# A gated-expert block with a LoRA feed-forward: one scale per expert for the gated rows, and another order of the first six items

## The chip, the cores and the metric

One core of a Trainium2 chip. The metric is the device time of one execution, in microseconds (us).

## What is computed

2048 rows x of 512 floats. Each row's token id picks one of four experts; every expert is a 512x512 matrix, used three times (as gate, as up and as down weight):

```python
n = layernorm(x)
z = n @ ct[e].T                        # gate and up weights are the same matrix
y = (silu(z) * z) @ ct[e]
x = x + tanh(g_xattn) * y              # "the gated rows" are silu(z) * z
n2 = layernorm(x)
x = x + tanh(g_ffn) * (n2 @ W_base + b_base + (n2 @ A_s) @ B_s
                       + sum over the top 2 of 6 routed experts of gate * ((n2 @ A_r) @ B_r))
```

The four expert matrices ("ct" in the kernel) come as 4 MB of floats, the feed-forward weights as 1.26 MB ("w") and 0.23 MB ("up").

## The kernel before

Five engines run lists of instructions written out by hand; semaphores tie them together. Each engine issues strictly in the order of its list.

The rows are sorted by expert, in three steps. VectorE counts and ranks the ids, GpSimd and VectorE build one-hot tiles (L1004, L410), and TensorE multiplies them into a table of row numbers (L684, copied at L1007). 16 tiles of 128 rows, and three extra items for experts that begin inside a tile, give 19 items. Item q is gathered by an indirect DMA that GpSimd issues (L404) into its 512 columns of `xg`.

Every float operand is split into a high and a low f16 part, and a product is three passes: hi x hi and hi x lo (L745, 8 matmuls) and lo x hi (L750, 4 matmuls), each 128x512. For this the operands are scaled by powers of two.

An item goes through: statistics on VectorE (`first_rows`: L1032, L1036); `item_root` on GpSimd (L373, L376, L383), which gives 1/sqrt(var) and the centre; `norm` on ScalarE (L538) into h; for items 0 to 5 `transpose_h` on TensorE (L736) with `hT_hi` on ScalarE (L511) and `hT_lo` on VectorE (L1049), from item 6 (`DMA_FROM`) on `h_hi` (L545), `h_lo` (L1054) and a DMA transpose issued by SyncE (L302); `product_z`; `silu_of` on ScalarE (L522); `activate` on VectorE (L1060), which multiplies silu(z), z and a scale and also sums each row; `scale_rows` (L1066 to L1070), which turns the row's sum into one scale per row (and `y_scale`, which takes it out again); `act_hi` on ScalarE (L529) and `act_lo` on VectorE (L1075), which write the split gated rows; a DMA transpose (L306); `product_y`; and `add_product` on VectorE (L1085, L1087), which adds y times `y_scale` to xg. z alternates between two PSUM banks, y between two others; h, silu and act are single buffers. act_split has two, hT and actT three.

Expert matrices: each arrives in `ct_stage` (1 MB, SyncE, L297; the fourth is issued only after the second gather). Its power of two comes from a sum of squares: for expert 0 from ScalarE (L497), for the others from `gram` on TensorE and `trace` on VectorE (L702, L942); `total` (L709) sums over partitions and `ct_scales` (L949 to L955) makes the scale and `z_scale`. Then `ct_hi` (ScalarE, L503) and `ct_lo` (VectorE, L935) write the two f16 halves of each half matrix. `z_scales` (GpSimd, L391 to L398) spreads `z_scale` over items 4 to 18.

The order around the change: GpSimd issues three gathers, then after `item_root(n)` one gather for n = 0, 1, 2 and two for each n from 3 on. From item 6 on TensorE alternates `product_z(q)` and `product_y(q - 2)` in a loop; ScalarE, VectorE and SyncE have loops that match. The feed-forward weights are loaded from ScalarE's queue (L548), into the space of `ct_stage` that the experts have left, at items 3 to 7. In the loop they are squared, scaled and split. After item 18 comes the feed-forward stage, 16 tiles: TensorE runs 24 matmuls (L727, L731) and the small low-rank ones for each.

`keep_warm` (L691) issues matmuls whose result nobody reads. `act_table` loads (L491, L646) switch ScalarE's function table; the last one stands between `silu_of(18)` and `act_hi(18)`.

## Time and profile before

| | |
|---|---|
| times of three runs | 215.31, 216.76, 218.06 us, median 216.76 |
| the profiled execution | 217.67 us, of which the span of instructions is 215.8 us |
| mean granted TensorE clock | 0.97 of full |
| busy in the span | TensorE 187.3 us (87%), VectorE 158.0 (73%), GpSimd 115.8 (54%), ScalarE 113.8 (53%) |

The profiled execution is one of its own, 0.91 us above the median; the span is its part between the first and the last instruction, and 1.87 us lie around it. A timeline row gives start, duration, engine, line and operation; in brackets stands how long the engine was idle before it, and what released it. "PE" is TensorE, "DVE" VectorE, "ACT" ScalarE, "POOL" GpSimd, "SP" SyncE.

### The profile page before, as it was taken

What the parts mean: (1) busy time and instruction counts of PE and PEld (TensorE: products, weight loads), DVE (VectorE), ACT (ScalarE), POOL (GpSimd) and SP (SyncE); (2) the same over time, 40 slices, a digit from 0 to 9 for tenths busy, and PEclk for the clock granted to TensorE, in tenths of its full rate; (3) what the DMA queues carried; (4) which work ended last, traced back from release to release, by engine and by line L of the source; (5) the groups of instructions that cost most, each with busy time, mean ns of one, the idle gap of its engine ahead of it and who ended that gap; (6) DMA issues with size and microseconds to landing.
All of it is one profiled execution on the core that took longest, in us unless ns stands there. A gap on an engine that the chain in (4) does not pass through costs nothing.

```text
span 215.8 us, 3806 instructions
## 1 busy us (share of the span) xinstructions
PE 187.3 (87%) x1076; PEld 109.2 (51%) x1076; DVE 158.0 (73%) x500; ACT 113.8 (53%) x208; POOL 115.8 (54%) x187
## 2 busy tenths in 40 slices
PE   0499686849994999999999999979999999999870
PEld 0374242314442444544444444637787787787650
DVE  4878496494696669999987994749878878876360
ACT  4445535634464567556665752636657757757210
POOL 4666552688768111116787533142677667776421
PEclk9999887879999999999999999999999999999997
DMA  3986103426999994449979976243389788889942
GB/s 104 380 258 234 49 3 97 111 81 110 189 228 285 251 155 97 97 97 164 256 206 231 149 189 172 53 121 75 61 136 149 104 137 130 122 121 142 121 63 86
DMA packets 58771, 31.37 MB, mean 145 GB/s; under 512 B 52049, under 2 KB 52049, under 8 KB 58754
## 3 DMA queue, kind: packets, MB, share of 16 engines
q1 hardware_dynamic: 53232, 16.80, 39.0%
q0 software_dynamic: 4816, 12.85, 27.9%
q10 hardware_dynamic: 706, 1.52, 2.1%
q8 instruction: 8, 0.13, 0.3%
q14 instruction: 9, 0.07, 0.1%
HBM read 10.71 MB, written 7.86 MB: 86 GB/s over the span
## 4 chain that ended last, share of the span: by engine, by line
PE 67%; DVE 10%; POOL 7%; DMA 4%; issue 4%; ACT 3%; POOLq 1%; SPq 1%; DVEq 0%
PE y_ps L745 6%; PE ffn_b L745 6%; PE z_ps L745 6%; PE actT_ps L745 6%; PE ffn_b L727 5%; PE ffn_a L727 5%; PE z_ps L750 3%; PE actT_ps L750 3%; PE y_ps L750 3%; PE ffn_b L750 3%; PE z_ps L727 3%; PE y_ps L727 2%; PE ffn_b L731 2%; PE ffn_a L731 2%; DMA hT<-h_split 2%
## 5 line engine op out<-in xcount | busy, mean ns | idle before, releaser
L461 POOL DMA_INDIRECT out<-scaled,row_index x14 | 22.4, 1597 | 9.1 <-POOL centre L450 4.6
L373 POOL TENSOR_SCALAR var_eps<-item_stats_t 128x1 f32<-128x1 f32 x19 | 6.4, 337 | 38.4 <-DVE item_stats_t L1036 37.8
L529 ACT ACTIVATE act_split<-act,row_scale 128x512 f16<-128x512 f32 x19 | 13.7, 721 | 21.0 <-DVE row_scale L1069 21.0
L745 PE MATMUL z_ps<-ct_split,hT 128*128 (+1 forms) x80 | 20.3, 400 | 4.2 <-DMA hT<-h_split 3.4
L423 POOL DMA_INDIRECT out<-xg,row_index x14 | 15.5, 1110 | 15.7 <-DVE xg L1087 13.1
L404 POOL DMA_INDIRECT xg<-x_rows,row_index x19 | 20.7, 1091 | 4.9 <-issue 3.8
L745 PE MATMUL ffn_b<-ct_split,hT 128*128 (+1 forms) x72 | 19.8, 425 | 3.4 <-DVE ct_split L935 3.4
L538 ACT ACTIVATE h<-xg,item_centre,item_rstd 128x512 f32<-128x512 f32 x18 | 14.5, 805 | 10.8 <-POOL item_centre L383 10.5
L745 PE MATMUL y_ps<-ct_split,actT 128*128 (+1 forms) x80 | 18.9, 379 | 1.1 <-DMA actT<-act_split 1.1
L727 PE MATMUL ffn_b<-w_split,hT 128*128 128x314 f16 x88 | 18.4, 295 | 0.9 <-ACT scaled L578 0.9
L727 PE MATMUL ffn_a<-w_split,hT 128*128 128x316 f16 x88 | 18.8, 298 | 0.0
L745 PE MATMUL actT_ps<-ct_split,actT 128*128 (+1 forms) x72 | 17.0, 379 | 0.0
L554 ACT ACTIVATE h<-xg,centre,rstd 128x512 f32<-128x512 f32 x16 | 12.8, 802 | 7.8 <-POOL centre L450 7.8
L1203 DVE TENSOR_TENSOR h_split<-h,h_split 128x512 f16<-128x512 f32 x16 | 10.7, 667 | 7.1 <-ACT h_split L559 7.1
L745 PEld LDWEIGHTS z_ps<-ct_split,hT 128*128 128x128 f16 x80 | 7.9, 102 | 14.7 <-issue 6.7
L563 ACT ACTIVATE expd<-logits,neg_max 128x6 f32<-128x6 f32 x16 | 4.8, 299 | 19.4 <-DVE neg_max L1221 19.4
L745 PEld LDWEIGHTS ffn_b<-ct_split,hT 128*128 128x128 f16 x72 | 7.6, 107 | 14.5 <-issue 4.3
L443 POOL TENSOR_SCALAR var_eps<-stats 128x1 f32<-128x1 f32 x16 | 7.3, 454 | 13.2 <-DVE stats L1039 13.1
L1075 DVE SCALAR_TENSOR_TENSOR act_split<-act,row_scale,act_split 128x512 f16<-128x512 f32 x19 | 14.1, 744 | 0.0
L745 PEld LDWEIGHTS y_ps<-ct_split,actT 128*128 128x128 f16 x80 | 7.8, 98 | 10.7 <-issue 1.6
L1032 DVE BATCH_NORM_STATS2 bn<-xg 128x6 f32<-128x512 f32 x19 | 13.0, 687 | 0.0
L935 DVE SCALAR_TENSOR_TENSOR ct_split<-ct_stage,ct_scale,ct_split 128x1024 f16<-128x1024 f32 x8 | 10.1, 1273 | 3.0 <-ACT ct_split L503 3.0
(203 smaller groups left out, 480.7 us busy)
## 6 DMA issues: line engine op xcount, KB each, us to landing
ct_stage<-ct SPq DMA_DIRECT2D x4, 1024.0 KB, 7.3
ct_stage<-w_ffn ACTq DMA_DIRECT2D x4, 315.0 KB, 3.7
hT<-h_split SPq DMA_TRANSPOSE x29, 3.4
xg<-x_rows,row_index POOLq DMA_INDIRECT x19, 4.3
actT<-act_split SPq DMA_TRANSPOSE x19, 3.4
out<-xg,row_index POOLq DMA_INDIRECT x16, 3.8
ct_stage<-w_up ACTq DMA_DIRECT2D x1, 224.0 KB
out<-scaled,row_index POOLq DMA_INDIRECT x14
```

Source lines behind the costliest of these rows:

```text
L404: nc.gpsimd.indirect_dma_start(cols(xg, q), None, x, bass.IndirectOffsetOnAxis(row_index[:, q:q + 1], 0)).then_inc(x_landed[q], 16)
L423: nc.gpsimd.indirect_dma_start(out, bass.IndirectOffsetOnAxis(row_index[:, q:q + 1], 0), cols(xg, q), None).then_inc(x2_stored, 16)
L461: nc.gpsimd.indirect_dma_start(out, bass.IndirectOffsetOnAxis(row_index[:, q:q + 1], 0), scaled[t % 3][:], None, compute_op=ALU.add).then_ ...
L529: nc.scalar.activation(act_split[q % 2][:, 0:D], act[:], ACT.Copy, scale=column(row_scale, q)).then_inc(act_hi_ready, 1)
L538: nc.scalar.activation(h[:], cols(xg, q), ACT.Identity, bias=column(item_centre, q), scale=column(item_rstd, q)).then_inc(h_ready, 1)
L554: nc.scalar.activation(h2[:], cols(xg, tile_position(l)), ACT.Identity, bias=centre[:], scale=rstd[:]).then_inc(h2_ready, 1)
L727: nc.tensor.matmul(ps, h2T[turn][:, k], rhs(part), start=(k == 0 and part == 0), stop=False)
L745: nc.tensor.matmul(ps[:], lhs[:, k], expert_weights(key, k, part), start=(k == 0 and part == 0), stop=False)
L750: last = nc.tensor.matmul(ps[:], lhs[:, KC + k], expert_weights(key, k, 0), start=False, stop=(k == KC - 1))
L1032: nc.vector.bn_stats(bn[:], cols(xg, q)).then_inc(bn_ready, 1)
L1075: nc.vector.scalar_tensor_tensor(act_split[q % 2][:, D:], act[:], column(row_scale, q), act_split[q % 2][:, 0:D], ALU.mult, ALU.subtract). ...
L1203: tt(h2_split[l % 3][:, D:], h2[:], h2_split[l % 3][:, 0:D], ALU.subtract).then_inc(h2_lo_ready, 1)
```

## The change

One scale per expert for the gated rows. `activate` multiplies by `act_scale`, a power of two made from the expert's own, and has no row sum; `scale_rows` is gone; `act_hi` and `act_lo` need no scale; `y_scale` comes once, for all items, from four more instructions on GpSimd in `scale_tables` (before: `z_scales`), which now runs after root 4 in place of root 5. `ct_scales` has two instructions in place of five, and `product_scales` makes the two product scales apart from it. `act_scale` of items 4 to 18 comes in one VectorE instruction, `late_act_scales`.

A new order, on all engines, of what comes before the loop. Four gathers are issued before root 0; after the roots 0 to 5 come 0, 1, 3, 3, 0 and 1 gathers, after the later ones two. VectorE builds 12 of the 16 one-hot tiles in place of 11. The first `total` goes to another bank (`hT_ps`) and does not wait for the row table. `transpose_act(q)` from q = 3 on waits until `product_y(q - 3)` is done.

The feed-forward weights get buffers of their own, and SyncE loads them between its transposes. The feed-forward stage and the loop from item 6 are otherwise as before. The diff, cut:

```diff
-w_stage = ct_stage[:, 0:2].rearrange("p s k n -> p (s k n)")[:, 0:KC * WN]
-up_stage = ct_stage[0:LORA + 1, 2, 0, :]
+w_stage = sb("w_stage", [P, KC * WN])
+up_stage = sb("up_stage", [LORA + 1, D])
...
-DVE_ONEHOTS = TPP - 5
+DVE_ONEHOTS = TPP - 4
...
     def transpose_act(q):
         sp.wait_ge(act_lo_ready, q + 1)
+        if q >= 3:
+            sp.wait_ge(y_done, q - 2)
         sp.dma_start_transpose(actT[q % 3][:], act_split[q % 2][:]).then_inc(actT_landed[q % 3], 16)
...
-    for q in range(1, ITEMS + 1):
+    def load_w(k):
+        sp.dma_start(cols(w_stage, k, WN), w_ffn[k * P:(k + 1) * P, :]).then_inc(w_loaded[k], 16)
+    transpose_act(0)
+    load_w(0)
+    transpose_act(1)
+    load_w(1)
+    transpose_act(2)
+    load_w(2)
+    transpose_act(3)
+    transpose_h(DMA_FROM)
+    load_w(3)
+    transpose_act(4)
+    transpose_h(DMA_FROM + 1)
+    sp.dma_start(up_stage[0:LORA], w_up[0:LORA]).then_inc(up_loaded, 16)
+    sp.dma_start(up_stage[LORA:], w_up[LORA:]).then_inc(up_loaded, 16)
+    for q in range(DMA_FROM, ITEMS):
         transpose_act(q - 1)
-        if q == DMA_FROM - 1:
-            transpose_h(DMA_FROM)
-            transpose_h(DMA_FROM + 1)
-        if DMA_FROM <= q < ITEMS - 2:
+        if q + 2 < ITEMS:
             transpose_h(q + 2)
-        if q >= ITEMS - 2:
+        else:
             transpose_h2(q + 2 - ITEMS)
+    transpose_act(ITEMS - 1)
+    transpose_h2(2)
...
+        pool.wait_ge(z_table_ready, 1)
+        nc.gpsimd.tensor_scalar(z_power[:], z_scale[:], 2.0 ** Z_TOP, None, ALU.mult).then_inc(z_table_step, 1)
+        pool.wait_ge(z_table_step, S + 3)
+        nc.gpsimd.tensor_tensor(z_square[:], z_power[:], z_power[:], ALU.mult).then_inc(z_table_step, 1)
+        pool.wait_ge(gate_mask_ready, 1)
+        nc.gpsimd.tensor_tensor(gated_power[:], z_power[:], gate_mask[:], ALU.mult).then_inc(z_table_step, 1)
+        pool.wait_ge(z_table_step, S + 5)
+        nc.gpsimd.tensor_tensor(y_scale[:], z_square[:], gated_power[:], ALU.mult).then_inc(y_scale_ready, 1)
...
     gather(2)
+    gather(3)
...
-        if n == 5:
-            z_scales()
-        for q in range(next_gather, min(ITEMS, next_gather + (2 if n >= 3 else 1))):
+        if n == 4:
+            scale_tables()
+        for q in range(next_gather, min(ITEMS, next_gather + (0, 1, 3, 3, 0, 1)[min(n, 5)] + (n > 5))):
             gather(q)
...
     def act_hi(q):
-        act_e.wait_ge(row_scale_ready, q + 1)
+        act_e.wait_ge(act_ready, q + 1)
         if q >= 2:
             act_e.wait_ge(actT_landed[(q - 2) % 3], landings(0, q - 2))
-        nc.scalar.activation(act_split[q % 2][:, 0:D], act[:], ACT.Copy, scale=column(row_scale, q)
-                             ).then_inc(act_hi_ready, 1)
+        nc.scalar.activation(act_split[q % 2][:, 0:D], act[:], ACT.Copy).then_inc(act_hi_ready, 1)
...
     ct_hi(0, 0)
     ct_hi(0, 1)
     ct_hi(1, 0)
+    ct_hi(1, 1)
     hT_hi(0)
-    ct_hi(1, 1)
+    ct_hi(2, 0)
     norm(1)
-    ct_hi(2, 0)
     hT_hi(1)
+    norm(2)
     silu_of(0)
     ct_hi(2, 1)
     act_hi(0)
-    norm(2)
-    silu_of(1)
     hT_hi(2)
-    act_hi(1)
     norm(3)
     ct_hi(3, 0)
     ct_hi(3, 1)
+    silu_of(1)
+    hT_hi(3)
+    norm(4)
+    act_hi(1)
     silu_of(2)
-    hT_hi(3)
+    hT_hi(4)
     act_hi(2)
-    norm(4)
     silu_of(3)
-    hT_hi(4)
+    norm(5)
     act_hi(3)
-    act_e.wait_ge(ct_lo_ready, 3)
-    load_w(0)
-    norm(5)
     silu_of(4)
     hT_hi(5)
+    norm(6)
     act_hi(4)
-    load_w(1)
-    norm(6)
     h_hi(6)
     silu_of(5)
     norm(7)
+    h_hi(7)
     act_hi(5)
-    h_hi(7)
-    load_w(2)
...
-    pe.wait_ge(rows_ready, 1)
+    def total_of(first, count):
+        return squares_ps[:, TOTALS_AT + first:TOTALS_AT + first + count]
     pe.wait_ge(ct_squared, 2)
-    total(0, 1, ct_squares[:, 0:1], ct_squares[:, S:S + 1])
+    total(first_total_ps[:, 0:1], ct_squares[:, 0:1], ct_squares[:, S:S + 1])
...
     product_z(0, 0, between=lambda: transpose_h(1))
+    gram(3)
     pe.wait_ge(ct_lo_ready, 2)
     product_z(1, 1)
-    gram(3)
+    transpose_h(2)
     pe.wait_ge(traced, 3)
-    total(3, 1, ct_squares[:, 3:4])
-    transpose_h(2)
+    total(total_of(3, 1), ct_squares[:, 3:4])
     pe.wait_ge(ct_lo_ready, 3)
     product_z(2, 2)
-    product_y(0, 0, between=lambda: transpose_h(3))
+    transpose_h(3)
+    product_y(0, 0)
     pe.wait_ge(ct_lo_ready, S)
-    product_z(3, 3)
-    product_y(1, 1, between=lambda: transpose_h(4))
+    product_z(3, 3, between=lambda: transpose_h(4))
     pe.wait_ge(tables_ready, 1)
     keys = {0: 0, 1: 1, 2: 2, 3: 3, 4: key_of(4), 5: key_of(5)}
     product_z(4, keys[4])
-    product_y(2, 2, between=lambda: transpose_h(5))
+    transpose_h(5)
+    product_y(1, 1)
     product_z(5, keys[5])
+    product_y(2, 2)
     product_y(3, 3)
...
-        after(ts(ct_exponent[:, at], squares_ps[:, TOTALS_AT + first:TOTALS_AT + first + count].bitcast(I32),
-                 23, None, ALU.logical_shift_right))
-        after(ts(ct_power[:, at], ct_exponent[:, at], -0.5, S_FIELD, ALU.mult, ALU.add))
-        ts(ct_scale[:, at], ct_power[:, at], 23, None, ALU.logical_shift_left).then_inc(ct_scale_ready, count)
-        dve.wait_ge(ct_scale_ready, first + count)
-        after(ts(ct_inverse[:, at], ct_scale[:, at], -1.0, BITS_OF_ONE_TWICE, ALU.mult, ALU.add))
-        ts(z_scale[:, at], ct_inverse[:, at].bitcast(F32), 2.0 ** -H_POWER, None, ALU.mult
+        after(ts(ct_root[:, at], total.bitcast(I32), 24, 23, ALU.logical_shift_right, ALU.logical_shift_left))
+        ts(ct_scale[:, at], ct_root[:, at], -1.0, float(S_FIELD << 23), ALU.mult, ALU.add
+           ).then_inc(ct_scale_ready, count)
+    def product_scales(first, count):
+        at = slice(first, first + count)
+        ts(z_scale[:, at].bitcast(I32), ct_root[:, at], 1.0, float(Z_FIELD << 23), ALU.mult, ALU.add
            ).then_inc(z_scale_ready, count)
+        ts(act_scale[:, at].bitcast(I32), ct_root[:, at], -1.0, float(ACT_FIELD << 23), ALU.mult, ALU.add
+           ).then_inc(act_scale_ready, count)
+    def late_act_scales():
+        dve.wait_ge(z_table_ready, 1)
+        ts(act_scale[:, S:].bitcast(I32), z_scale[:, S:].bitcast(I32), -1.0,
+           float((ACT_FIELD + Z_FIELD) << 23), ALU.mult, ALU.add).then_inc(act_scale_ready, 1)
...
     def activate(q):
         dve.wait_ge(silu_ready, q + 1)
+        dve.wait_ge(act_scale_ready, min(q, S) + 1)
         if q:
             dve.wait_ge(act_lo_ready, q)
-        nc.vector.scalar_tensor_tensor(act[:], z_banks[q % 2][:], column(z_scale, q), silu[:], ALU.mult,
-                                       ALU.mult, accum_out=column(row_sum, q)).then_inc(act_ready, 1)
-    def scale_rows(q):
-        dve.wait_ge(act_ready, q + 1)
-        ts(column(row_mean, q), column(row_sum, q), 2.0 ** -ROW_POWER, 2.0 ** -100, ALU.mult, ALU.max
-           ).then_inc(row_mean_ready, 1)
-        dve.wait_ge(row_mean_ready, q + 1)
-        nc.vector.reciprocal(column(row_scale, q), column(row_mean, q)).then_inc(row_scale_ready, 1)
-        ts(column(y_scale, q), column(row_mean, q), column(gate_mask, q), column(z_scale, q), ALU.mult, ALU.mult
-           ).then_inc(y_scale_ready, 1)
+        nc.vector.scalar_tensor_tensor(act[:], z_banks[q % 2][:], column(act_scale, q), silu[:], ALU.mult,
+                                       ALU.mult).then_inc(act_ready, 1)
     def act_lo(q):
         dve.wait_ge(act_hi_ready, q + 1)
-        nc.vector.scalar_tensor_tensor(act_split[q % 2][:, D:], act[:], column(row_scale, q),
-                                       act_split[q % 2][:, 0:D], ALU.mult, ALU.subtract
-                                       ).then_inc(act_lo_ready, 1)
+        tt(act_split[q % 2][:, D:], act[:], act_split[q % 2][:, 0:D], ALU.subtract).then_inc(act_lo_ready, 1)
...
     def add_product(q):
         dve.wait_ge(y_done, q + 1)
-        dve.wait_ge(y_scale_ready, q + 1)
+        dve.wait_ge(y_scale_ready, 1)
...
     gates_of_rows()
+    product_scales(0, 1)
     ct_lo(0, 0)
-    first_rows(0)
+    ct_lo(0, 1)
     trace(1)
     trace(2)
-    ct_scales(1, 2, 2)
+    first_rows(0)
+    ct_scales(squares_ps[:, TOTALS_AT + 1:TOTALS_AT + 3], 1, 2, 2)
     first_norm()
     first_rows(1)
-    ct_lo(0, 1)
+    first_rows(2)
+    ct_lo(1, 0)
     hT_lo(0)
-    ct_lo(1, 0)
     ct_lo(1, 1)
+    ct_lo(2, 0)
+    first_rows(3)
+    activate(0)
     hT_lo(1)
-    activate(0)
-    scale_rows(0)
-    first_rows(2)
-    ct_lo(2, 0)
+    trace(3)
     act_lo(0)
-    trace(3)
     ct_lo(2, 1)
-    ct_scales(3, 1, 3)
+    ct_scales(squares_ps[:, TOTALS_AT + 3:TOTALS_AT + 4], 3, 1, 3)
     hT_lo(2)
+    product_scales(1, 3)
+    first_rows(4)
+    ct_lo(3, 0)
     activate(1)
-    scale_rows(1)
-    first_rows(3)
-    act_lo(1)
-    ct_lo(3, 0)
-    first_rows(4)
-    activate(2)
-    scale_rows(2)
     ct_lo(3, 1)
     hT_lo(3)
+    first_rows(5)
+    act_lo(1)
+    activate(2)
+    act_lo(2)
+    hT_lo(4)
+    activate(3)
+    first_rows(6)
+    act_lo(3)
+    late_act_scales()
+    activate(4)
+    hT_lo(5)
     add_product(0)
-    act_lo(2)
-    first_rows(5)
-    activate(3)
-    scale_rows(3)
-    hT_lo(4)
-    first_rows(6)
+    h_lo(6)
     add_product(1)
-    act_lo(3)
-    activate(4)
-    scale_rows(4)
-    hT_lo(5)
     first_rows(7)
+    act_lo(4)
     add_product(2)
-    act_lo(4)
-    h_lo(6)
+    activate(5)
+    h_lo(7)
     first_rows(8)
-    activate(5)
-    scale_rows(5)
-    h_lo(7)
```

## Rows read from the trace of the kernel before

**Rows 1.** Windows by stage: busy us of each engine, clock, DMA share, GB/s
```profile
20.52:67.89 47.37, 35.60 (x159) 16.22 (x159) 32.98 (x76) 23.56 (x33) 29.99 (x44) 0.89 0.51 116
67.89:145.30 77.41, 76.32 (x365) 35.78 (x366) 60.07 (x160) 43.08 (x64) 32.97 (x58) 1.00 0.75 164
145.30:204.00 58.70, 57.81 (x438) 45.31 (x437) 46.39 (x181) 37.09 (x96) 37.05 (x51) 1.00 0.79 118
```

**Rows 2.** Waits of TensorE, 68 us to the end: us in total, times, longest
```profile
PE z_ps L745 <- DMA hT<-h_split: 3.4, 1, 3.4
PE y_ps L745 <- DMA actT<-act_split: 1.1, 1, 1.1
```

**Rows 3.** Timeline of TensorE: start us, us, line, operation, count, idle before it
```profile
35.12 3.26 PE L745 MATMUL z_ps<-ct_split,hT 128*128 128x512 f16 x8 [0.78 <-ACT hT L511]
...
45.94 3.46 PE L745 MATMUL ffn_b<-ct_split,hT 128*128 128x512 f16 x8 [3.36 <-DVE ct_split L935]
...
67.89 1.90 PE L745 MATMUL z_ps<-ct_split,hT 128*128 x8 [3.39 <-DMA hT<-h_split]
...
73.08 1.89 PE L745 MATMUL ffn_b<-ct_split,hT 128*128 x8
...
75.67 1.89 PE L745 MATMUL actT_ps<-ct_split,actT 128*128 x8
```

**Rows 4.** Timeline of VectorE in the start-up, same columns
```profile
19.21 1.25 DVE L935 SCALAR_TENSOR_TENSOR ct_split<-ct_stage,ct_scale,ct_split 128x1024 f16<-128x1024 f32 x1
20.38 0.69 DVE L1049 TENSOR_TENSOR hT<-hT_ps,hT 128x512 f16<-128x512 f32 x1
20.98 2.47 DVE L935 SCALAR_TENSOR_TENSOR ct_split<-ct_stage,ct_scale,ct_split 128x1024 f16<-128x1024 f32 x2
...
27.23 0.75 DVE L1060 SCALAR_TENSOR_TENSOR act<-z_ps,z_scale,silu 128x512 f32<-128x512 f32 x1 [0.63 <-ACT silu L522]
...
28.21 0.16 DVE L1069 RECIPROCAL row_scale<-row_mean 128x1 f32<-128x1 f32 x1
...
28.46 0.68 DVE L1032 BATCH_NORM_STATS2 bn<-xg 128x6 f32<-128x512 f32 x1
```

**Rows 5.** Timeline of GpSimd in the start-up
```profile
21.27 2.23 POOL L383 TENSOR_SCALAR item_centre<-item_stats_t,item_rstd 128x1 f32<-128x1 f32 x1
...
32.95 1.03 POOL L404 DMA_INDIRECT xg<-x_rows,row_index  x1 [0.17 <-issue]
...
39.19 0.26 POOL L383 TENSOR_SCALAR item_centre<-item_stats_t,item_rstd 128x1 f32<-128x1 f32 x1
...
49.89 1.43 POOL L391 TENSOR_SCALAR z_scale_of<-item_key,z_scale 128x15 f32<-128x15 f32 x4
```

**Rows 6.** Timeline of ScalarE in the start-up
```profile
26.51 0.69 ACT L522 ACTIVATE silu<-z_ps,z_scale 128x512 f32<-128x512 f32 x1 [0.64 <-PE z_ps L750]
...
39.48 0.81 ACT L538 ACTIVATE h<-xg,item_centre,item_rstd 128x512 f32<-128x512 f32 x1 [1.98 <-POOL item_centre L383]
40.20 2.17 ACT L503 ACTIVATE ct_split<-ct_stage,ct_scale 128x1024 f16<-128x1024 f32 x2
```

**Rows 7.** The page, section 6: DMA issues, median us to landing
```profile
xg<-x_rows,row_index POOLq DMA_INDIRECT x19, 4.3
actT<-act_split SPq DMA_TRANSPOSE x19, 3.4
```

**Rows 8.** Line L404, 13.3 to 14 us: the gather of item 2
```profile
L404 POOL DMA_INDIRECT xg<-x_rows,row_index x1: 946/946/946, 13.4 to 13.4; - x1
...
DMA to landing us min/median/max: 6.6/6.6/6.6
```

**Rows 9.** Line L306, all transposes of the gated rows: landing
```profile
DMA to landing us min/median/max: 2.7/3.4/6.2
```

**Rows 10.** Timeline of ScalarE at the last expert item
```profile
136.51 1.28 ACT L646 ACT_TABLE_LOAD   x1
137.80 0.72 ACT L529 ACTIVATE act_split<-act,row_scale 128x512 f16<-128x512 f32 x1
```

More of the change, by code:

```diff
@@ L191, in build_block @@
         squares_ps = ffn_a[1]
+        first_total_ps = hT_ps
         TOTALS_AT = 0
@@ L384, in item_root, with scale_tables @@
                                             column(item_rstd, n), ALU.mult, ALU.mult).then_inc(rstd_ready, 1)
-            def z_scales():
+            def scale_tables():
                 pool.wait_ge(z_scale_ready, S)
@@ L425, in store_x2 @@
                 ).then_inc(x2_stored, 16)
[L427 removed]
+            next_gather, next_store = 4, 0
             for n in range(ITEMS):
@@ L704, in gram, with total @@
                 last.then_inc(gram_done, 1)
-            def total(first, count, *parts):
+            def total(to, *parts):
                 for n, part in enumerate(parts):
-                    last = nc.tensor.matmul(squares_ps[:, TOTALS_AT + first:TOTALS_AT + first + count], ones_f32[:],
-                                            part, start=(n == 0), stop=(n == len(parts) - 1))
+                    last = nc.tensor.matmul(to, ones_f32[:], part, start=(n == 0), stop=(n == len(parts) - 1))
                 last.then_inc(ct_totalled, 1)
-            pe.wait_ge(rows_ready, 1)
+            def total_of(first, count):
+                return squares_ps[:, TOTALS_AT + first:TOTALS_AT + first + count]
             pe.wait_ge(ct_squared, 2)
-            total(0, 1, ct_squares[:, 0:1], ct_squares[:, S:S + 1])
+            total(first_total_ps[:, 0:1], ct_squares[:, 0:1], ct_squares[:, S:S + 1])
             gram(1)
@@ L719, in _ @@
             keep_warm(WARM_UP[1])
+            pe.wait_ge(rows_ready, 1)
             pe.wait_ge(traced, 2)
-            total(1, 2, ct_squares[:, 1:3])
+            total(total_of(1, 2), ct_squares[:, 1:3])
             keep_warm(WARM_UP[2])
@@ L943, in trace, with ct_scales @@
                                                ALU.mult, accum_out=column(ct_squares, e)).then_inc(traced, 1)
[L945 removed]
+            def ct_scales(total, first, count, turn):
                 at = slice(first, first + count)
                 dve.wait_ge(ct_totalled, turn)
[L949 to L956 removed]
+                after(ts(ct_root[:, at], total.bitcast(I32), 24, 23, ALU.logical_shift_right, ALU.logical_shift_left))
[4 more added lines that the diff above has]
+                ts(z_scale[:, at].bitcast(I32), ct_root[:, at], 1.0, float(Z_FIELD << 23), ALU.mult, ALU.add
+                   ).then_inc(z_scale_ready, count)
+                ts(act_scale[:, at].bitcast(I32), ct_root[:, at], -1.0, float(ACT_FIELD << 23), ALU.mult, ALU.add
[4 more added lines that the diff above has]
+                   float((ACT_FIELD + Z_FIELD) << 23), ALU.mult, ALU.add).then_inc(act_scale_ready, 1)
             def reach(slots):
@@ L1014, in _ @@
             cp(key_table[:], item_key[:]).then_inc(tables_ready, 1)
-            ct_scales(0, 1, 1)
+            ct_scales(first_total_ps[:, 0:1], 0, 1, 1)
             def gates_of_rows():
@@ L1023, in gates_of_rows @@
                 dve.wait_ge(gates_ready, 1)
-                after(ts(gate_mask[:], gate_mask[:], gates_t[:, 0:1], 2.0 ** H_POWER, ALU.mult, ALU.mult))
+                ts(gate_mask[:], gate_mask[:], gates_t[:, 0:1], 0.5, ALU.mult, ALU.mult).then_inc(gate_mask_ready, 1)
             def item_stats(q):
```

38 lines of the change are left out of this document (12 added, 26 removed).

## The prediction

> **What bounds the kernel now.** First I read busy time by stage. From 67.89 us on TensorE is busy for 76.3 of 77.4 us and then for 57.8 of 58.7 us; between 20.52 and 67.89 us it is busy for only 35.6 of 47.4 us, at a mean clock of 0.89 [rows 1]. The waits of TensorE behind 68 us are 3.4 us once, which ends at 67.89, and 1.1 us near 142 us [rows 2]. So from z6 (the first product of the loop, at 67.89) to the end the kernel is a row of matmuls, and a gain must come from the time at which z6 starts. In the loop a product takes 75.67 - 73.08 = 2.59 us [rows 3]. By 67.89 ten have run (z0 to z5, y0 to y3), 26 us of work.
>
> Then the timelines of the start-up, to see what TensorE waits for. z2 starts at 35.12 behind item 2's transposes, z3 at 45.94 behind the low half of expert 3, both at half clock: 3.26 and 3.46 us for eight matmuls that take 1.89 at full clock [rows 3]. Behind both lies item_root: the gather of item 3 is issued only at 32.95 [rows 5], so its statistics come late and `norm(3)` starts at 39.48; `ct_hi(3)` stands behind it on ScalarE and starts at 40.20 [rows 6]. The start-up is a ring of gather, statistics, root, norm with one gather in each turn.
>
> GpSimd is slow inside that ring. `item_centre` takes 0.26 us when nothing is in its way, and 2.23 us at 21.27, where it ends with the two `ct_lo` that VectorE runs from 20.98 for 2.47 us [rows 4, 5]. The Trainium skill (GPSIMD Engine Reference, "Key points") says that GpSimd shares its SBUF interfaces with VectorE and is in contention with VectorE instructions that have two SBUF inputs; `ct_lo` is one, and the trace agrees. By that page alone GpSimd would run clear of `activate`, which reads a PSUM bank; I can do without it, since the sum below only lets a GpSimd instruction that begins within a `ct_lo` or `act_lo` wait for its end, as in the rows.
>
> **The parts with small effect.** The row table: GpSimd makes four one-hots in place of five, the table is ready some 0.3 us earlier. The first `total` no longer waits for it; with three instructions fewer in `ct_scales`, expert 0's scale is ready about 0.8 us earlier. In the steady loop, VectorE loses the row sum and three short instructions for each item, about 0.5 us of its 5.2, and `act_hi` can start about 0.4 us sooner after `activate` (27.23 + 0.75 to 28.4, past the reciprocal at 28.21 [rows 4]). TensorE bounds that stretch [rows 1], so that is worth nothing there. At item 18, where TensorE does wait for the gated rows (1.1 us [rows 2]), `act_hi` starts at 137.80 because the table load of 1.28 us ends then [rows 10]; so there too I take 0, with 0.4 as the bound. The waits on `y_done` in SyncE's list are met long before: 0. Four short GpSimd instructions are added to `scale_tables`; four of the kind take 1.43 us [rows 5]; I take 1.2 us, on the path of root 5.
>
> **The new start-up, step by step.** Durations: `ct_hi` 1.08 each, norm 0.81, silu 0.69 [rows 6], `ct_lo` 1.25, `hT_lo` 0.69 (0.6 until the next starts), statistics 0.82, `activate` 0.75 [rows 4]; `hT_hi` 0.6, `act_hi` and `act_lo` 0.66, transposes 0.45 to 0.66, as their neighbours in the timeline; a free root 0.2 + 0.57 + 0.26 and gaps, 1.25; a gather 1.03 on GpSimd, 1.3 with its gap [rows 5], and 3.5 to 6.6 until it lands (median 4.3) [rows 7, 8]; a transpose by DMA 2.7 to 6.2, median 3.4 [rows 7, 9].
>
> 1. Item 0's statistics now stand behind two `ct_lo` and two traces (about 16.4), its norm still ends by 17.8, since root 0 is free. `first_rows(2)` stands ahead of `ct_lo(1, 0)`. The gather of item 2 was issued beside the fourth expert load and took 6.6 us, to 19.96 [rows 8]. So VectorE waits for it until about 19.6; it is done at 20.45.
> 2. That wait leaves GpSimd clear: root 1 ends at 19.9, not at 23.5. norm(1) follows `ct_hi(2, 0)`, 20.6 to 21.4. z0 runs at 19.6 and is done at 23.9, 2.6 us early.
> 3. Root 2 falls into `ct_lo(1, 1)` and `ct_lo(2, 0)`, and ends with them at 24.8. norm(2) ends at 25.65, and only then ScalarE comes to `silu_of(0)`: `activate(0)` at 26.4 (was 27.23), `act_lo(0)` done at 28.8.
> 4. Three gathers follow root 2 (25.0 to 28.5); root 3, though its statistics are there at 25.6, waits for them and for `ct_lo(2, 1)`: 31.05. norm(3) ends at 31.9 (was 40.3), `ct_hi(3)` at 34.0. This is where most of the gain arises.
> 5. z1 28.6, z2 30.0 to 32.7, y0 33.1 to 35.7. `activate(1)` 34.75, `ct_lo(3, 1)` done 36.65; z3 at 36.7 (was 45.94).
> 6. Three more gathers, 31.2 to 35.2; root 4 meets `ct_lo(3, 1)`: 37.5. norm(4) ends 38.35, z3 39.7, `act_lo(1)` 39.7, `hT_hi(4)` 40.3, z4 43.3.
> 7. `scale_tables` on GpSimd: 37.5 to 42.0 (1.43 and 0.6 as before, 1.2 new, about 1 lost to `act_lo`); root 5 43.2, norm(5) 44.0, transposes of item 5 44.5.
> 8. From there TensorE has all it needs: y1, z5, y2, y3 are 4 x 2.59 = 10.4 us, 44.5 to 54.9. Beside it root 6 (45.8), norm(6), `act_hi(4)`, `h_hi(6)`, `h_lo(6)` (48.6) and the DMA transpose, landed 51.4 to 54.9 with 2.7 to 6.2. It is hidden, but at the slow end only just.
> 9. z6 at about 55.0, where it was at 67.89. Then every 5.2 us an item, as before; the transpose of item 7 is issued at about 54 and wanted at 60.
>
> The weights' loads leave ScalarE's list, cost SyncE about 0.4 us each and stand there ahead of transposes that come microseconds later. The DMA page of the Trainium skill (DMA: Bandwidth & Descriptors, "Issuing engines are not separate DMA queues") says that the issuing engine does not matter, since all run on the same 16 engines and interleave. By it the move to SyncE is worth 0; no row here shows a load in the transposes' own queue. I take 0 from the rows too: transposes have landed in 6.2 us at worst beside gathers and loads.
>
> **The sum.** 67.89 - 55.0 = 12.9 us. A step list of this kind leaves out late landings and half-clock products; the clock was at 1.2 GHz after two of the gaps [rows 3] and cost 1.4 and 1.6 us in the eight matmuls behind each. Gaps of 1 us before z2 and z3 remain. I take 1 us for it: 11.9 us. From the profiled 217.67 that gives 205.8; against the median of 216.76 it is 204.9. I forecast 205.0. Bounds of the unknown: all transposes at 6.2 and all roots caught by one more `ct_lo` (1.25 each for roots 3, 4 and 5) give z6 at about 60 and 210; z6 at 53 (no tables' delay, 2 us) gives 202.5. The forecast's own range is 202 to 208.5.
>
> About 2% is what a measurement of this kernel can tell from no change: 4.3 us, a time below 212.4.
>
> **Rivals.**
> *GpSimd becomes the bound* (0.17). Six gathers stand ahead of roots 3 and 4, each of 1.3 us, and `scale_tables` ahead of root 5. For it: GpSimd is busy 30 of 47 us in the old start-up [rows 1], its instructions stretch from 0.26 to 2.23. Against: the old root 3 came at 39, with slack of 8 us over mine. If each of roots 3 to 6 ends 1.25 to 1.5 us later: 5 to 6 us, 210.
> *Half clock through the dense stretch* (0.10). z0 to z4 come with gaps; if TensorE is at 1.2 GHz when y1 starts, each product costs up to 2.59 us more. For one to two products 3 to 5 us: 208 to 210. Against: z3 and z4 keep it busy for most of 36.7 to 43.3.
> *The order does nothing* (0.05): z6 waits for its DMA transpose behind gathers and weight loads that now crowd the same stretch. DMA share was 0.51 in the start-up and 0.75 in the loop [rows 1]; moving 0.24 x 47 = 11 us of transfer ahead of z6 would use up the gain: 216.
> *Slower* (0.03): the second rival carried on. All four products from 44.5 to z6 at 1.2 GHz put z6 at 56 + 10.4 = 66.4, and if z6 and z7 then come in late from their DMA transposes and the clock stays low, each further item of two products costs 5.2 us more: 71.6 after one, 76.8 after two, where 67.89 stood before. It decides at the second item of the loop; with that one too it is 8.9 us later than before, 226.
> *The forecast* 0.65.
>
> **How the numbers follow.** 205.0 is the likeliest. The range runs from 202.0, below which nothing in the list goes, to 211.0, past the first two rivals. Faster by over 2%: 0.65 + 0.17 + 0.09 = 0.91; within 2%: 0.06; slower: 0.03.
>
> **What would show it.** Right: TensorE's matmul L745 of z6 near 55 us, z3 near 37, norm(3) near 31, GpSimd gathers three in a row at 25 and 31 us, and from z6 on the same 2.59 us and the same wait of about 1 us before y18. The span ends 12 us earlier, the loop and the feed-forward stage last as long as before. Wrong: a wait of z6 or z7 for hT over 2 us (DMA), L745 groups of 3.4 us behind 44 us (clock), or roots 3 and 4 later than 34 and 40 us (GpSimd).

## The result, and the profile after

The changed kernel takes 207.0 us (median of 4 runs, 206.63 to 208.81), where the kernel before took 217.31 (median of 4). The ratio is 0.956, 95% interval 0.947 to 0.965: 4.4% faster. Most kernels here have some executions that take over 1.5% longer than their fastest one; a median takes these in, a ratio and its interval leave them out. I had forecast 205.0 us in a range of 202 to 211. The profiled execution after took 207.26 us with a span of 205.4, against 217.67 and 215.8: 10.4 us less. VectorE is busy 146.1 us (was 158.0), TensorE 183.5 (was 187.3).

TensorE in the start-up and at the two places where it waits later (start, duration, line, operation, idle time before it):

```profile
24.63 1.89 PE L756 MATMUL ffn_b<-ct_split,hT 128*128 128x512 f16 x8
...
29.79 1.89 PE L756 MATMUL z_ps<-ct_split,hT 128*128 128x512 f16 x8 [0.66 <-ACT hT L533]
...
36.19 1.90 PE L756 MATMUL ffn_b<-ct_split,hT 128*128 128x512 f16 x8 [0.62 <-DVE ct_split L948]
...
43.27 0.66 PE L747 MATMUL hT_ps<-ident,h 128*128 128x128 f32 x4 [0.28 <-ACT h L559]
43.76 1.89 PE L756 MATMUL actT_ps<-ct_split,actT 128*128 128x512 f16 x8
...
54.12 1.89 PE L756 MATMUL z_ps<-ct_split,hT 128*128 x8
```
```profile
62.90 1.90 PE L756 MATMUL actT_ps<-ct_split,actT 128*128 x8 [0.85 <-DMA actT<-act_split]
...
131.61 2.46 PE L756 MATMUL y_ps<-ct_split,actT 128*128 x8 [2.08 <-DMA actT<-act_split]
133.86 1.91 PE L761 MATMUL y_ps<-ct_split,actT 128*128 x4
```

These answer to [rows 3]. z2 starts at 29.79 (was 35.12), z3 at 36.19 (was 45.94), both at full clock: eight matmuls in 1.9 us, not 3.3 and 3.5. From 43.76, y1, z5, y2 and y3 run without a gap, and z6 starts at 54.12, where it was 67.89. That is 13.8 us, more than the 10.4 of the whole. So 3.4 us are lost again behind z6. The two waits show where to look: `actT_ps` (y5) at 62.90 and `y_ps` (y18) at 131.61, both on a transpose of gated rows. The same in windows, cut at z6, z18 and the first feed-forward matmul behind y18 (columns as [rows 1]):

```profile
20.52:54.12 33.60, 29.43 (x155) 14.32 (x154) 26.75 (x46) 19.37 (x29) 26.63 (x41) 1.00 0.70 172
54.12:118.38 64.26, 63.17 (x293) 28.61 (x292) 47.60 (x93) 38.05 (x57) 29.48 (x51) 1.00 0.86 168
118.38:135.56 17.18, 15.11 (x73) 7.33 (x72) 8.29 (x21) 7.21 (x11) 5.24 (x11) 0.92 0.52 107
```

From z6 to z18 the kernel before took 130.42 - 67.89 = 62.53 us, which is the bare work: 24 products of 2.59 us, and 0.36 us of small matmuls. Now it is 64.26. The balance of the profiled executions, each term a difference of two starts:

| stretch | before | after | gain |
|---|---|---|---|
| to z6 | 67.89 | 54.12 | +13.77 |
| z6 to z18 | 62.53 | 64.26 | -1.73 |
| z18 to y18 | 12.24 | 13.23 | -0.99 |
| y18 to the next feed-forward matmul | 2.60 | 3.95 | -1.35 (half clock) |
| from there to the end of the span | 70.54 | 69.84 | +0.70 |

GpSimd, VectorE and ScalarE in the start-up, as [rows 4 to 6]:

```profile
19.48 0.27 POOL L398 TENSOR_SCALAR item_centre<-item_stats_t,item_rstd 128x1 f32<-128x1 f32 x1
...
22.46 2.22 POOL L398 TENSOR_SCALAR item_centre<-item_stats_t,item_rstd 128x1 f32<-128x1 f32 x1
24.85 1.03 POOL L425 DMA_INDIRECT xg<-x_rows,row_index  x1 [0.17 <-issue]
26.18 0.95 POOL L425 DMA_INDIRECT xg<-x_rows,row_index  x1 [0.30 <-issue]
27.43 0.95 POOL L425 DMA_INDIRECT xg<-x_rows,row_index  x1 [0.30 <-issue]
...
30.39 0.26 POOL L398 TENSOR_SCALAR item_centre<-item_stats_t,item_rstd 128x1 f32<-128x1 f32 x1
```
```profile
19.56 0.69 DVE L1054 BATCH_NORM_STATS2 bn<-xg 128x6 f32<-128x512 f32 x1 [1.12 <-DMA xg<-x_rows,row_index]
...
22.16 2.47 DVE L948 SCALAR_TENSOR_TENSOR ct_split<-ct_stage,ct_scale,ct_split 128x1024 f16<-128x1024 f32 x2
...
26.14 0.75 DVE L1083 SCALAR_TENSOR_TENSOR act<-z_ps,act_scale,silu 128x512 f32<-128x512 f32 x1 [0.69 <-ACT silu L544]
```
```profile
30.69 0.81 ACT L559 ACTIVATE h<-xg,item_centre,item_rstd 128x512 f32<-128x512 f32 x1 [1.04 <-POOL item_centre L398]
```

The statistics of item 2 wait 1.12 us for their gather at 19.56; `item_centre` of item 1 beside them takes 0.27 us. That of item 2, at 22.46, ends with the two `ct_lo` of 2.47 us, 2.22 us later. This is how a reader finds the contention: here, as in the rows before the change, the short instruction ends where the long one of the other engine ends. Then come three gathers in a row, root 3 at 30.65, and norm(3) at 30.69, where it was 39.48.

### The profile page after: what moved, and what is told of

Read it like the earlier page. It is cut to its first block, busy times and chain, and to the rows that moved or that the text cites. A ratio compares the mean times of both kernels' runs of the same rounds, so it can differ in the third digit from the quotient of the medians.

```text
span 205.4 us, 3746 instructions
## 1 busy us (share of the span) xinstructions
PE 183.5 (89%) x1076; PEld 107.5 (52%) x1076; DVE 146.1 (71%) x421; ACT 112.2 (55%) x208; POOL 114.7 (56%) x190
## 4 chain that ended last, share of the span: by engine, by line
PE 62%; POOL 12%; DMA 8%; DVE 5%; issue 5%; ACT 4%; SPq 1%; POOLq 1%; ACTq 0%
PE y_ps L756 6%; PE actT_ps L756 6%; DMA actT<-act_split 5%; PE ffn_b L738 5%; PE ffn_b L756 5%; PE ffn_a L738 5%; PE z_ps L756 4%; POOL xg L425 4%; PE y_ps L761 3%; PE actT_ps L761 3%; DMA ct_stage<-ct 3%; PE z_ps L738 3%; PE y_ps L738 3%; PE ffn_b L761 3%; PE ffn_b L742 2%
## 5 line engine op out<-in xcount | busy, mean ns | idle before, releaser
L425 POOL DMA_INDIRECT xg<-x_rows,row_index x19 | 20.2, 1064 | 5.3 <-issue 4.2
L756 PE MATMUL y_ps<-ct_split,actT 128*128 (+1 forms) x80 | 19.5, 387 | 2.1 <-DMA actT<-act_split 2.1
L388 POOL TENSOR_SCALAR var_eps<-item_stats_t 128x1 f32<-128x1 f32 x19 | 6.7, 351 | 24.7 <-DVE item_stats_t L1058 24.0
L756 PE MATMUL z_ps<-ct_split,hT 128*128 (+1 forms) x80 | 18.9, 379 | 1.6 <-DVE act L1083 0.7
L738 PE MATMUL ffn_b<-w_split,hT 128*128 128x314 f16 x88 | 18.5, 297 | 0.0
L551 ACT ACTIVATE act_split<-act 128x512 f16<-128x512 f32 x19 | 11.9, 626 | 11.4 <-DVE act L1083 11.4
L756 PE MATMUL ffn_b<-ct_split,hT 128*128 (+1 forms) x72 | 17.0, 379 | 0.6 <-DVE ct_split L948 0.6
L1088 DVE TENSOR_TENSOR act_split<-act,act_split 128x512 f16<-128x512 f32 x19 | 13.0, 683 | 2.3 <-ACT act_split L551 2.3
L391 POOL TENSOR_TENSOR item_rstd<-var_eps,minus_half 128x1 f32<-128x1 f32 x19 | 12.0, 632 | 1.6
L742 PE MATMUL ffn_b<-w_split,hT 128*128 128x314 f16 x44 | 11.9, 296 | 0.0
```

The lines of the kernel that those rows point to most:

```text
L391: nc.gpsimd.tensor_tensor(column(item_rstd, n), var_eps[:], minus_half[:], ALU.pow).then_inc(rstd_ready if n == 0 else pool_step, 1)
L425: nc.gpsimd.indirect_dma_start(cols(xg, q), None, x, bass.IndirectOffsetOnAxis(row_index[:, q:q + 1], 0)).then_inc(x_landed[q], 16)
L738: nc.tensor.matmul(ps, h2T[turn][:, k], rhs(part), start=(k == 0 and part == 0), stop=False)
L742: return nc.tensor.matmul(ps, h2T[turn][:, KC + k], rhs(0), start=False, stop=(k == KC - 1))
L756: nc.tensor.matmul(ps[:], lhs[:, k], expert_weights(key, k, part), start=(k == 0 and part == 0), stop=False)
L1088: tt(act_split[q % 2][:, D:], act[:], act_split[q % 2][:, 0:D], ALU.subtract).then_inc(act_lo_ready, 1)
```

## The experiments

Most change one thing; c1, c4 and d1 change two together, and b2 builds on b1. A time is the median; where the comparison gives one, the ratio to the kernel before, run beside it on the same chip, stands with it. That kernel's medians were 219.2 us beside a1, a2, a3 and a5, 221.3 beside a4, b1 and b2, and 218.4 beside the c kernels and beside d1, so I compare ratios, and starts of products (z6, y5, z18, y18) within profiles.

### Which part of the change makes the gain

**a1, the old order with the new scale.** The scale's instructions of the diff, in the old lists.

```diff
-                after(ts(ct_exponent[:, at], ...
+                after(ts(ct_root[:, at], ...
...
-            scale_rows(0)
...
+            late_act_scales()
             activate(4)
```

> The kernel before with the one scale per expert alone, in the old order (the scale tables stand behind root 4, as they must). My theory says the order brings the gain: TensorE bounds the loop, so only the three activations that stand on the old start-up's chain (items 0, 1 and 2) each save 0.4 to 0.5 us, and the tables cost some of it on root 5. z6 at 66 to 67 us, 215 to 217 us, ratio 0.99 to 1.00. Rival: the scale itself makes the gain, since VectorE loses 10 us of work in all: ratio below 0.975.

Measured: 216.67 us, ratio 0.988 (0.982 to 0.994). So the scale alone gives 1.2%, about 2.6 us, a little more than I expected and far from the rival's 2.5%. Its profiled execution took 222.7 us, 6 us above its median, so it can't say where the 2.6 us arise. It has z5 at 57.51 (was 59.15), but z6 only at 70.44, behind a wait of 7.6 us for its transpose, much as in a5 below.

**a2, the new order with the old scale.**

```diff
-                nc.vector.scalar_tensor_tensor(act[:], ..., column(act_scale, q), silu[:], ALU.mult, ALU.mult)
+                nc.vector.scalar_tensor_tensor(act[:], ..., column(z_scale, q), silu[:], ALU.mult, ALU.mult, accum_out=...)
...
             activate(0)
+            scale_rows(0)
```

> The changed kernel with the scale per row put back (row sum, three short instructions and act_hi behind them), all else as changed. Theory: worth little in the loop; in the start-up activate stands on the way to act_lo(0), act_lo(1), act_lo(2), which are not the latest, so z6 moves from 54.1 to 55 or 56 and the time to 208 or 209. Rival, that the new order works only with the shorter VectorE list: z6 at 58 or later, above 211 us.

Measured: 209.42 us, z6 at 54.72. The rival falls: the new order does not need the shorter VectorE list. The medians on that chip give 209.42 / 219.17 = 0.956, as the changed kernel's, but with no interval, and the four runs lie between 205.56 and 209.79. So what the scale is worth in the new order is not resolved here; z6 moved by 0.6 us.

**a5, the old order with early statistics.** Two moves on VectorE, nothing else.

```diff
             ct_lo(0, 1)
+            first_rows(2)
             hT_lo(0)
...
+            first_rows(3)
             activate(0)
             scale_rows(0)
-            first_rows(2)
...
             scale_rows(1)
-            first_rows(3)
```

> The kernel before with two moves on VectorE alone: the statistics of items 2 and 3 ahead of the waits on ScalarE (before hT_lo(0) and before activate(0)). Theory: in the old order each item's statistics stood behind the activation of two items earlier, and that made the ring; taken out, root 2 comes 3 us earlier, norm(3) 4 to 6 us earlier, z6 near 63 to 64, 212 to 213.5 us. Rival, that the one gather in each turn of the ring is what spaces the items: root 3 stays where it is and the time within 1 us of before.

Measured: 215.7 us, ratio 0.972 (0.963 to 0.982). The ring does break here, with the gathers left as they were: z2 starts at 30.62 (was 35.12), z3 at 39.76 (was 45.94), z5 at 53.10 (was 59.15). But z6 came only at 66.36, not at the 63 to 64 I expected. It waits 7.9 us for its transpose:

```profile
PE z_ps L745 <- DMA hT<-h_split: 7.9, 1, 7.9
```
```profile
55.71 1.97 SPq L306
...
57.73 8.37 DMA hT<-h_split
...
66.36 3.59 PE z_ps L745 x8
```

The second fence is the chain, in order of time: the transpose of item 4's gated rows is issued from SyncE's queue, then at 57.73 the one for z6's hT, which lands 8.37 us later, then z6 runs at half clock.

**d1, the same with the weight loads moved out of that stretch.**

```diff
-        W_SQUARE_AT = W_LOAD_AT + KC + 1
+        W_SQUARE_AT = 9
...
-            load_w(0)
...
+                if q in (DMA_FROM, DMA_FROM + 1):
+                    load_w(2 * (q - DMA_FROM))
+                    load_w(2 * (q - DMA_FROM) + 1)
+                if q == 9:
                     act_e.dma_start(up_stage[0:LORA], ...
```

> The kernel before with the statistics of items 2 and 3 early, as in the earlier run of that, and the weight loads of ScalarE's queue moved out of the start-up: none before z6's transpose is issued, two each at items 6 and 7, squares at item 9, up at item 9. In the earlier run z5 came 6 us sooner but z6 only 1.5 us, behind a transpose that took 8.4 us to land. Theory A: the loads and gathers on the DMA engines took the gain back; without the loads that transpose lands in 4 to 6 us and z6 is at 61 to 64. Theory B: the old order itself leaves only 3 us between h_lo(6) and the end of y3, so z6 waits 3 to 4 us whatever the loads do, and it can't come below 61. A and B together: z6 at 61 to 63, waiting 3 to 4 us, and 211 to 213.5 us. If the loads do not matter z6 stays at 66 and the time at 214 to 216.

Measured: 211.37 us, ratio 0.968 (0.960 to 0.976). z6 at 60.22, behind a wait of 3.3 us.

```profile
PE z_ps L743 <- DMA hT<-h_split: 3.3, 1, 3.3
```

That is nearly as A and B together had it (z6 at 61 to 63, a wait of 3 to 4): two moves and the loads bring z6 7.7 of the 13.8 us forward, and a wait of 3.3 us stays, as long as the one in [rows 2]. Of the 6.1 us against a5, 2.3 are an earlier issue (55.40 against 57.73; 1.6 of them because z3 ran at full clock, where in a5 its eight matmuls took 3.51 us), and 3.8 a shorter landing (4.6 us). The intervals of a5 and d1 overlap, so that the loads matter here rests on these two profiles (one execution each), with c1 below.

**a3, the gathers one or two at a time.**

```diff
-next_gather + (0, 1, 3, 3, 0, 1)[min(n, 5)] + (n > 5)
+next_gather + (0, 1, 1, 2, 2, 2)[min(n, 5)]
```

> The changed kernel with 0, 1, 1, 2, 2, 2 gathers behind roots 0 to 5 and two from then on, in place of 0, 1, 3, 3, 0, 1. Theory: the three gathers behind root 2 keep root 3 waiting for 3 us; with one, root 3 ends near 27 or 28 in place of 30.65, norm(3) and z3 follow by 1 to 3 us, and the gathers left over crowd the loop a little: z6 at 52 to 54, 205 to 207.5 us. Rival: the threes are needed, items 6 to 8 come late without them, z6 or z7 waits, 208 to 211 us.

Measured: 209.3 us, ratio 0.952 (0.946 to 0.959): by time the same as with threes. Root 3 ends at 27.66 as expected, 3 us sooner, but norm(3) starts at 30.05, only 0.6 us sooner:

```profile
27.55 0.62 ACT L551 ACTIVATE act_split<-act 128x512 f16<-128x512 f32 x1
29.56 0.60 ACT L533 ACTIVATE hT<-hT_ps 128x512 f16<-128x512 f32 x1 [1.39 <-PE hT_ps L747]
30.05 0.80 ACT L559 ACTIVATE h<-xg,item_centre,item_rstd 128x512 f32<-128x512 f32 x1
```

ScalarE stands in `hT_hi(2)`, which waits for TensorE, until 30.05. That instruction itself ran 0.5 us later than in the changed kernel (29.56, there 29.05), so the three gathers cost about 1 us and not 3. In exchange gathers fall on the transposes later: the one issued at 45.17 took 9.3 us, y3 waited 2.2 us, and z6 came at 57.16, not at the 52 to 54 I expected. In this profile the rival is right.

**c4, item 6 late again.**

```diff
-            transpose_h(5)
             product_y(1, 1)
+            transpose_h(5)
...
-            h_lo(6)
             add_product(1)
             first_rows(7)
             act_lo(4)
+            h_lo(6)
```

> The changed kernel with item 6 made late again: the fifth item's transposes behind y1 on TensorE, and h_lo(6) behind the next add, the statistics of item 7 and act_lo(4) on VectorE. Theory: the second half of the gain is that item 6's chain (root, norm, h_hi, h_lo, DMA transpose) now starts 10 us of products ahead of z6; with h_lo(6) ending near 53 in place of 47.9, its transpose lands at 57 to 60 and z6 waits 3 to 6 us, so 3 to 5 us slower than the changed kernel. Rival: z6 is set by the products in front of it and takes the shift with less than 1 us.

Measured: 210.37 us, ratio 0.980 (0.968 to 0.992). Against the changed kernel on the same chip (c0, below) that is 2.7 us more by the medians and 4.7 by the ratios. The size came, but not by my mechanism. `h_lo(6)` ended near 50.6, not 53, since nothing it was put behind had to be waited for, and z6 started at 54.63. Behind it y4 waited 1.8 us and z7 0.6: the transposes of items 4, 6 and 7 now follow one another within 4 us.

### What takes 3.4 us back behind z6

**a4, the loads back on ScalarE's queue**, at the old places, with the new buffers.

```diff
             act_hi(3)
+            load_w(0)
...
             transpose_act(0)
-            load_w(0)
             transpose_act(1)
-            load_w(1)
```

> The changed kernel with the feed-forward weights loaded from ScalarE's queue at the old places (behind act_hi of items 3 to 7), the separate buffers kept. Theory: the queue does not matter, and the loads come at the same stretch of the loop; y5's transpose, which took 6.5 us to land and cost 0.85 us, stays late or gets later since more of the loads fall beside it. 207 to 208 us, same within 0.5%. Rival: loads ahead of transposes in one queue hold them up: y5's wait goes and 205.5 to 206.

Measured: 206.85 us, ratio 0.946 (0.933 to 0.958); z6 at 53.72, y5 without a wait, z7 and z8 late by 1.0 and 0.5 us. By time, no difference that can be told. This does not test the queue by itself: at the old places all loads come 5 to 12 us later, the fourth weight load at 58.55 (49.19 in the changed kernel) and the up load at 64.19 (55.05). That y5 no longer waits fits the queue, as the rival had it, and fits the later loads as well; c1 below moves the loads within SyncE's list.

**b1, the feed-forward root ahead of the stores** on GpSimd.

```diff
             for n in (1, 2, 3):
+                tile_root(n)
                 for t in range(next_store, min(SUMMED, next_store + 2)):
                     store_x2(t)
                     next_store = t + 1
-                tile_root(n)
```

> The changed kernel with one thing more on GpSimd: at the end of the expert items each feed-forward root stands ahead of the two stores and not behind them. Theory: the 2.1 us wait before y18 comes from a store that waits for VectorE's add at 118.6 and holds the root, by it ScalarE's norm at 122.4 and by that silu of item 18, though z18 was done at 121.0. With the root first silu(18) starts near 121, y18's wait falls from 2.1 to under 0.5 us, and the clock doesn't fall behind it: 203.5 to 205.5 us. Rival: the wait is the slow landing of the transpose (4.2 us against 3.1 before), which stays: within 0.5 us of 207.

Measured: 207.72 us, ratio 0.952 (0.934 to 0.969); not the 203.5 to 205.5 us I expected, and too wide to tell by time. The profile tells the mechanism. After, then b1, ScalarE behind z18:

```profile
122.39 0.81 ACT L572 ACTIVATE h<-xg,centre,rstd 128x512 f32<-128x512 f32 x1 [4.27 <-POOL centre L472]
...
123.78 0.67 ACT L544 ACTIVATE silu<-z_ps,z_scale 128x512 f32<-128x512 f32 x1
124.46 1.28 ACT L660 ACT_TABLE_LOAD   x1
125.76 0.63 ACT L551 ACTIVATE act_split<-act 128x512 f16<-128x512 f32 x1
```
```profile
120.88 0.63 ACT L577 ACTIVATE h_split<-h 128x512 f16<-128x512 f32 x1
123.19 0.69 ACT L544 ACTIVATE silu<-z_ps,z_scale 128x512 f32<-128x512 f32 x1 [1.68 <-PE z_ps L761]
123.90 1.28 ACT L660 ACT_TABLE_LOAD   x1
125.19 0.63 ACT L551 ACTIVATE act_split<-act 128x512 f16<-128x512 f32 x1
```

In the changed kernel silu(18) starts at 123.78, 2.8 us after z18's end (at 120.97 the next product starts), behind the norm that waited for GpSimd. In b1 it starts at 123.19 with its idle time put down to TensorE: z18 of that execution ended at 123.0. y18 has no wait, so the 2.1 us before it go with the order of root and store. From the start of z18 to the end of the span it is 83.7 us in b1 and 87.0 in the changed kernel. The loop of that execution lost more, though (z6 to z18 65.65 us): y5 waited 1.4 us and z15 1.2. z15 waits as long in b2 (1.3) and 0.4 in c0; why is open.

**b2, b1 and the table load behind `act_hi(18)`.**

```diff
-                if q == ITEMS - 1:
-                    nc.scalar.preload_act_table(ACT.Exp)
                 act_hi(q)
+                if q == ITEMS - 1:
+                    nc.scalar.preload_act_table(ACT.Exp)
```

> As the root-first kernel, and ScalarE's table load moved behind act_hi(18). Theory: act_hi(18) no longer waits 1.28 us for the table, act_lo(18) comes up to 1 us earlier; if y18 waits no more in the root-first kernel it brings nothing more, if it still waits it brings up to 0.7 us. 203 to 205.5 us.

Measured: 206.72 us, ratio 0.947 (0.937 to 0.958). No wait before y18 either, and nothing that the interval could tell from b1; above the 203 to 205.5 I expected.

**c0, the changed kernel again**, as measure for c1, c2 and c4, which ran on the same chip.

> The changed kernel itself, for comparison on one chip with the three others. z6 near 54 us, a wait before y18 near 2 us, y5 between 0.4 and 2 us late; ratio 0.945 to 0.965.

Measured: 207.67 us, 205.34 to 208.72 over six runs, ratio 0.958 (0.950 to 0.967).

**c1, two loads later, with b1's root.** The squares of the weights come one item later too.

```diff
-        W_SQUARE_AT = 8
+        W_SQUARE_AT = 9
...
-            load_w(3)
...
-            sp.dma_start(up_stage[0:LORA], w_up[0:LORA]).then_inc(up_loaded, 16)
-            sp.dma_start(up_stage[LORA:], w_up[LORA:]).then_inc(up_loaded, 16)
...
+                if q == 7:
+                    load_w(3)
+                if q == 9:
+                    sp.dma_start(up_stage[0:LORA], ...
```

> The root-first kernel with the last two loads taken out of the crowded stretch: the fourth weight load behind item 9's transpose, the up load behind item 11's, the squares one item later. Theory: y5 (0.4 to 2.7 us late in all variants so far) and z8 wait since gathers, loads and transposes share the DMA engines between 48 and 62 us; without the two loads y5 and z8 are on time, z6 to z18 takes 62.5 to 63.5 us where it took 64.3 in the changed kernel, and with no wait before y18 the time is 3 to 5 us below the changed kernel on the same chip (ratio 0.93 to 0.945). Rival: the gathers and transposes alone fill the engines and the loads do not matter: y5 as late as before, gain only the 2 to 3 us of y18.

Measured: 203.41 us, 202.82 to 204.99 over six runs, ratio 0.945 (0.938 to 0.952). All six runs lie below all six of c0; the medians differ by 4.3 us, and what the ratios give is some 3 us. That is the 3 to 5 I expected, with the ratio at the upper end of my 0.93 to 0.945. This is the fastest kernel of the study. Its waits between z6 and z18, and those of c0 from z6 to behind y18:

```profile
PE z_ps L758 <- issue: 0.2, 1, 0.2
```
```profile
PE actT_ps L756 <- DMA actT<-act_split: 2.3, 1, 2.3
PE y_ps L756 <- DMA actT<-act_split: 2.1, 1, 2.1
```

z6 starts at 54.08, z18 at 117.22 (63.1 us later, 67.3 in c0's profile and 64.3 in the one shown first), y18 right behind y17: z18 to y18 takes 11.0 us in place of 13.2. How the time divides between the two changes no run here tells, since c1 has both and b1 ran on another chip.

**c2, all loads in one place**, ahead of `transpose_act(5)`.

```diff
             transpose_h(DMA_FROM + 1)
+            for k in range(KC):
+                load_w(k)
             sp.dma_start(up_stage[0:LORA], ...
```

> The changed kernel with all four weight loads and the up load issued one behind the other just ahead of the transpose of item 5's gated rows. Theory: 1.5 MB ahead of it on the same engines, about 4 us more until it lands; y5 3.5 to 6 us late, z8 too, 3 to 5 us slower than the changed kernel. Rival: loads do not hold transposes up, y5 no later than 1 to 2 us and the time the same.

Measured: 214.38 us, ratio 0.985 (0.976 to 0.993): 6.7 us above c0 by the medians, 5.7 by the ratios, where I had 3 to 5. y5 waits 5.2 us and then runs at half clock (3.59 us for its eight matmuls), which puts z8 2.5 us further back. Landing of the transpose of item 5's gated rows, line L306 in c0 and c1:

```profile
DMA to landing us min/median/max: 8.0/8.0/8.0
```
```profile
DMA to landing us min/median/max: 4.9/4.9/4.9
```

And SyncE's queue in c2, with the landing of that transpose:

```profile
55.94 2.02 SPq L313 DMA_DIRECT2D w_stage<-w_ffn  x4
...
58.90 2.28 SPq L306 DMA_TRANSPOSE actT<-act_split  x1
```
```profile
DMA to landing us min/median/max: 9.0/9.0/9.0
```

8.0 us in c0, 4.9 in c1 and 9.0 in c2. So two loads, 0.54 MB together, go with a landing that is 3.1 us longer and with a wait of 2 us. Moving all 1.5 MB there added only 1.0 us to the landing, where I had expected about 4; the larger part is SyncE's own list, which issues six transfers first and comes to the transpose at 58.90, 2.6 us later than in c0 (56.28). Together they cost some three-fifths of the change's gain.

## Why the prediction was right, and where it was off

Two rows of the kernel before, the gather of item 3 and its statistics, bear on the fourth point:

```profile
16.75 1.01 POOL L404 DMA_INDIRECT xg<-x_rows,row_index  x1 [0.31 <-POOL item_rstd L376]
```
```profile
36.84 0.68 DVE L1032 BATCH_NORM_STATS2 bn<-xg 128x6 f32<-128x512 f32 x1
```

- *The bound.* Right. All of the gain comes from the time at which z6 starts.
- *The new start-up, step by step.* Right within 1.3 us at every step. Root 2 at 24.7 (24.8 said), `activate(0)` 26.1 (26.4), root 3 30.65 (31.05), norm(3) done 31.5 (31.9), z3 36.2 (36.7), root 4 36.9 (37.5), the transposes of item 5 43.3 (44.5), z6 54.1 (55.0). The steps were early, not late, so the 1 us that I added "for late landings and half-clock products" was for nothing in this stretch: the clock stayed at its full level from 20.5 to 54 us.
- *Four short GpSimd instructions, 1.2 us.* They ran from 39.65 to 40.75: 1.1. And `scale_tables` lost less to `act_lo` than I gave it: it took 3.84 us in place of 4.5, and ended at 40.75 in place of 42.0.
- *The gather of item 3 is issued only at 32.95.* A misreading. Three gathers stand ahead of the roots, so the fourth, at 16.75, is item 3's, and that at 32.95 is item 5's. The rows of item 3 were there at 20.65, 16 us before their statistics. What held the ring was VectorE's list, which had those statistics behind the activation of item 1. a5 shows it: with the gathers as they were, z3 came 6.2 us sooner. It did no harm to the sum, which was made from the order of the lists.
- *Three gathers: "This is where most of the gain arises".* I had put norm(3)'s 8 us there. The gain at norm(3) is real (8.8 us) but owes to the early statistics; the threes themselves put norm(3) about 1 us later (a3), and by time they are worth nothing that could be told, though z6 was 3 us later without them in the one profile.
- *In the steady loop nothing, "Then every 5.2 us an item, as before".* This is the step that failed: the loop lost 1.73 us, mostly at y5 and z8. I had held z6's and z7's transposes against their due times and not those of the gated rows. y5's was issued at 56.11 and wanted at 61.9, 5.8 us later, and took 6.5. I had taken 6.2 as the worst from [rows 9]. That one was issued near 48 us in the old start-up, and the DMA share around it (47.5 to 54 us) was 0.72; around y5's (56.1 to 62.6 us) it is 1.09, by the profile's own count, which can pass 1.
- *The loads in SyncE's list, "I take 0"*. Not quite: each takes SyncE 0.58 to 0.67 us to issue, not 0.4, and in c1 y5's transpose, without a load in front of it, is issued at 55.80 and lands in 4.9 us.
- *"It is hidden, but at the slow end only just"* for z6. It landed 2.3 us ahead (issued 47.91, 3.9 us).
- *"The same wait of about 1 us before y18".* It was 2.1 us, in this profile and in those of a3, a4, c0, c2 and c4 (1.6 in a2). What it comes from in the first place was not in my list: the store that holds the root, and by it ScalarE (b1). The 1 us that came on top is all in the landing of the transpose: it is issued 8.9 us behind z18's start before the change and 8.8 after, and lands in 3.1 us before and 4.2 after. Why it lands later I can only argue: the add of item 16 now ends before `act_lo(18)`, and so its store (126.79) goes to the DMA engines ahead of the transpose (127.14), where before it came behind (139.41 and 139.34).
- *The scale, "worth nothing there".* In the new order nothing resolved (a2); in the old order 1.2% (a1), where I had said 0 to 1%.
- *The rivals.* GpSimd as the bound: no, roots 3 and 4 were early. Half clock: not in the dense stretch, but once behind y18, 1.35 us. The third, that DMA takes the gain back, I had put at z6 and at all of the gain; it struck three products later and took most of 1.7 us. Against the profiled execution I had 205.8, and it took 207.26: 1.9 us too little gain up to z6 (0.9 and the allowance of 1) against 3.4 us lost behind it. The rest of the 2 us between 205.0 and 207.0 is the step from profile to median: 0.91 us before, 0.26 after.

What stays open: how much of the last 6 us at z6 (60.2 in d1 to 54.1) is due to each of the moves on ScalarE, TensorE and VectorE that were not tried alone; how much of c1's gain is the loads' and how much the root's; and why executions with the same order up to there differ by 2 us at y5 (waits of 0.4 us in b2, 0.9 in the profile shown first, 1.4 in b1, 2.3 in c0).
